# Two streamed matmuls on TensorE ahead of the wait for a normalised input, in a post-norm decoder on one core

## The reference

```
x = _layernorm(x + L0_attn(x))        # 16 heads, Gaussian-splat weights, softmax
x = _layernorm(x + L0_xattn(x, ctx))  # 16 heads of 16, 120 context tokens
x = _layernorm(x + L0_ffn(x))         # 8 experts, the best one per token
x = _layernorm(x + L1_attn(x))        # causal, 16 heads of 16
x = _layernorm(x + L1_xattn(x, ctx))  # two attentions of 16 heads of 32, each with
                                      # its own norms, gains and a GELU layer 256-1024-256
x = _layernorm(x + L1_ffn(x))         # 16 small experts, the best four per token
```

## Time and profile before

| | |
|---|---|
| time, median of 3 runs | 3850.71 us (3845.12 to 3853.26) |
| profiled execution: its time | 3838.08 us |
| profiled execution: span from first to last instruction | 3836.4 us |
| mean granted TensorE clock | 0.916 of full |
| TensorE matmuls busy / weight loads busy | 86% / 61% of the span |
| VectorE, ScalarE, GpSimd busy | 72%, 55%, 25% |

### The profile page before, as it was taken

One profiled execution on the slowest core, in us unless ns is written; L12 is line 12 of the kernel. 1 busy time (PEld: TensorE's weight loads), 2 busy tenths in 40 slices (PEclk: granted clock), 3 DMA queues, 4 the chain that ended last, 5 costly groups with the idle time before them and its releaser, 6 DMA issues. The chain is left out here.

```text
span 3836.4 us, 94561 instructions
## 1 busy us (share of the span) xinstructions
PE 3284.4 (86%) x38960; PEld 2338.5 (61%) x38960; DVE 2751.5 (72%) x6299; ACT 2092.8 (55%) x4222; POOL 972.9 (25%) x1792
## 2 busy tenths in 40 slices
PE   1989888889888888988988888899988898988886
PEld 1666565666666656656656666566655665766654
DVE  5777776777776767777767667677776677777754
ACT  4745665455456564564465555645555556466552
POOL 0312341122223321131133122212342113124310
PEclk9999998999989999989989898898988999998987
DMA  5000000000000000000000000000000000000000
GB/s 168 3 3 2 2 3 5 10 8 3 2 2 4 5 3 7 7 3 2 7 2 2 5 4 8 6 4 2 2 2 3 10 7 6 2 2 2 2 4 6
DMA packets 30365, 31.49 MB, mean 8 GB/s; under 512 B 8673, under 2 KB 26482, under 8 KB 29938
## 3 DMA queue, kind: packets, MB, share of 16 engines
q1 hardware_dynamic: 29938, 25.44, 2.1%
HBM read 21.24 MB, written 4.19 MB: 7 GB/s over the span
## 5 line engine op out<-in xcount | busy, mean ns | idle before, releaser
L1116 ACT ACTIVATE p<-bank,p_log 128x512 f32<-128x512 f32 (+2 forms) x1280 | 746.8, 583 | 1225.3 <-PE bank L808 1174.7
L1690 POOL TENSOR_TENSOR prob<-p,prob 120x256 f16<-120x256 f32 (+2 forms) x512 | 452.6, 884 | 1727.6 <-ACT prob L1117 1726.5
L1117 ACT ACTIVATE prob<-bank,p_log 128x512 f16<-128x512 f32 (+2 forms) x1280 | 747.5, 584 | 0.0
L1392 DVE TENSOR_REDUCE negm<-bank 128x2 f16<-128x512 f32 (+1 forms) x1280 | 675.5, 569 | 24.8 <-PE bank L763 13.5
L1310 DVE TENSOR_TENSOR prob<-p,prob 128x512 f16<-128x512 f32 (+2 forms) x768 | 467.2, 616 | 169.6 <-ACT prob L1117 165.6
L785 PE MATMUL bank<-q,k 32*128 32x256 f16 (+2 forms) x6144 | 486.9, 284 | 69.6 <-ACT prob L1117 26.6
L675 PE MATMUL bank<-w_exp,ident_h 128*128 128x512 f16 x1280 | 418.7, 411 | 16.3 <-DVE xa L1304 11.9
L1699 POOL TENSOR_SCALAR_AFFINE_SELECT probm<-prob 128x128 f16<-128x128 f16 x1024 | 326.3, 357 | 316.4 <-DVE prob L1310 316.4
L785 PEld LDWEIGHTS bank<-q,k 32*128 32x128 f16 (+1 forms) x6144 | 303.5, 108 | 147.1 <-issue 41.4
L808 PE MATMUL bank<-ident_h,negm 128*128 128x256 f16 (+2 forms) x2560 | 376.8, 268 | 0.0
L1682 POOL TENSOR_TENSOR rstd<-veps,minus_half 128x2 f32<-128x2 f32 (+2 forms) x192 | 146.0, 760 | 813.5 <-DVE veps L1278 812.9
(11 more groups left out here) (302 smaller groups left out, 6211.6 us busy)
## 6 DMA issues: line engine op xcount, KB each, us to landing
x<-in_x SPq DMA_DIRECT2D x16, 256.0 KB, 2.7
out<-z SPq DMA_DIRECT2D x16, 256.0 KB, 2.1
xa<-in_li SPq DMA_DIRECT2D x9, 256.0 KB, 4.4
x<-in_li SPq DMA_DIRECT2D x7, 256.0 KB, 4.4
z<-in_wq SPq DMA_DIRECT2D x4, 256.0 KB, 4.1
z<-in_li SPq DMA_DIRECT2D x4, 256.0 KB, 4.6
cx<-in_ctx_t SPq DMA_DIRECT2D x16, 60.0 KB, 1.9
cx<-in_ctx SPq DMA_DIRECT2D x16, 60.0 KB, 1.8
```

The costliest lines, as they stand in the source:

```text
L1116: act(p32[0:n, g % PBUF32, 0:cols], ps[0:n, 0:cols], ACT.Exp, bias=p_log[0:n, :], scale=a.scale)
L1117: act(prob[0:n, 0, g % PBUF, 0:cols], ps[0:n, 0:cols], ACT.Exp, bias=p_log[0:n, :], scale=a.scale).then_inc(a_done, one(a_done))
L1392: v.tensor_reduce(negm[:, h * NT:(h + 1) * NT], ring_v[bank_of(e, v_full)][:, :].rearrange("p (t n) -> p t n", t=NT)[:, :, 0:ATTNS[k].keys ...
L1690: g.tensor_tensor(prob[0:n, 1, m % PBUF, 0:cols], p32[0:n, m % PBUF32, 0:cols], prob[0:n, 0, m % PBUF, 0:cols], ALU.subtract).then_inc(pp_ ...
```

## The change

`STREAM_NORM` goes from 0 to 2, and `transposes` uses it: when the source is a normalised activation, TensorE issues two streamed matmuls into the bank it has just taken, and only then waits for the first token tile. The four transposes overwrite the bank. The wait for the bank, in `slot`, still comes before the streamed matmuls.

```diff
-STREAM_NORM, STREAM_GATES, STREAM_HEADS, STREAM_ROWS = 0, 0, 0, 2
+STREAM_NORM, STREAM_GATES, STREAM_HEADS, STREAM_ROWS = 2, 0, 0, 2
...
                     if after is not None:
                         stream(ps, meanwhile)
                         e.wait_ge(*after)
+                    if normed is not None:
+                        stream(ps, STREAM_NORM)
                     for t in range(NT):
                         if normed is not None:
                             e.wait_ge(normed, upcoming(e, normed))
```

## The result

The kernel after the change takes 3865.56 us (median of 14 runs, 3854.29 to 3875.17), the one before 3850.52 us (14 runs). The ratio is 1.0032, 95% interval 1.0024 to 1.0040: slower by 0.32%, some 12 us, and clear of the 0.2% (the two medians are 15.0 us apart). Forecast were 3856 us, with "slower" as the likeliest of the three signs (0.39); the time lies inside the range, and in the upper half of the range given for the likeliest case. The rise was forecast at 5 us and is 12 to 15.

The account below looks back on a forecast made before the run. TensorE was taken as first suspect for the bound, but not alone. 25 us of exposed cost less 17 us of clock gain, less 2 us, gave +6 us; forecast 3856 us (+0.1%), range 3824 to 3888 us.

Parts of the forecast that it names:

- "slower": Whole kernel: the sign for a time above 3858 us, beyond 0.2% of 3851; chance 0.39.
- the likeliest case: Whole kernel: cost and clock gain nearly cancel, 3856 us, own range 3840 to 3874; chance 0.40.
- the sum: Whole kernel: 25 us cost less 17 us clock gain, less 2 us, giving +6 us.
- (a): Rival, calls without a norm wait: the cost is nearly all on the path, +33 us, 3884 us; chance 0.23.
- (b): Rival, behind the long waits: the clock decides, half the long falls go, -26 us, 3825 us; chance 0.21.
- (c): Rival, whole kernel: TensorE isn't the bound and the cost vanishes, -9 us, 3842 us; chance 0.16.
- The cost term: TensorE in calls without cover: 42.5 us of added work, of which 25 us reach the end.
- 70 calls without a norm wait: Calls whose transposes don't wait for the norm: 0.55 us a streamed pair, 38.5 us of TensorE.
- 0.6: Share of a microsecond added to TensorE that moves the end, where TensorE doesn't wait; read from the chain that ended last.
- the long waits: 30 waits of 1.6 to 4.0 us in "xT" of k = 4 and the tail: pair fits, direct cost 0.
- The clock term: TensorE behind norm waits: fewer falls to 1.2 GHz, 13 us (long waits) plus 4 us (short), 17 us gained.
- the short waits: At most 28 norm waits, 2 us or less: 4 us of pairs uncovered; 4 us clock gain from 15 of them.

Follow-up runs that it names:

- e10: The changed kernel, unedited, run again against the kernel before; ratio 1.0037 (1.0023 to 1.0051).
- e2: Changed kernel with two streamed matmuls only in the 96 calls other than "xT" of k = 4 and the tail, against the kernel before; 0.9998.
- e11: Changed kernel with two streamed matmuls only in the 64 calls of k = 1 to 3, against the kernel before; ratio 1.0021.
- e1: Changed kernel with two streamed matmuls only in the 32 "xT" calls of k = 4 and the tail, against the kernel before; ratio 1.0003.
- e3: Changed kernel with eight streamed matmuls only in the 32 "xT" calls of k = 4 and the tail, against the kernel before; ratio 0.9994.
- e9: The kernel before, unedited, as a kernel of its own against the runs of before; ratio 1.0010 (0.9994 to 1.0025).
- e8: Changed kernel with four streamed matmuls only in the 64 calls of k = 1 to 3, against the kernel before; ratio 1.0047.
- e5: Changed kernel with eight streamed matmuls only in the 16 "xT" calls of k = 4, against the kernel before; ratio 0.9999.
- e6: e3 with eight more streamed matmuls in the tail ahead of the wait for the gates, against the kernel before; ratio 0.9974.
- e12: e6 with four streamed matmuls in the 32 "xoT" calls as well, against the kernel before; ratio 1.0017.
- e4: Changed kernel with four streamed matmuls in all 128 calls, against the kernel before; ratio 1.0077.

## Why the prediction came out as it did

*The places of cost and gain.* Right in kind. The change costs TensorE time where no wait hides it and lifts the clock a little; both are in the profile after, and cost outweighs gain, as the sum said. No rival took over. (a) wanted +33 us, against 12 to 15 in the medians and 18.4 in the profile; (b) wanted the mean clock at 0.93, and it is 0.921; (c) wanted waits for other things to shrink, and they didn't.

*The cost term.* 25 us were taken. Once the clock is out, 25 are in the executions of e10, and 29 to 31 in the two profiles after. The total was right, its distribution wasn't, so that there is luck in it. I charged 70 calls without a norm wait alike, at 0.6, and the long waits nothing. By the table, two matmuls in the 64 early calls cost 15 us; their price is 64 x 0.55 = 35 us, less the 9.9 us that left the waits for `x` 25, so that 0.6 came out there. In the 32 "xoT" calls, 17.6 us at that price, they cost about 1 (e2 less e11). And pairs in the long waits, booked at a direct cost of 0, have 9 us in the table (e1), as a cost or as a clock that was worth less than its price. The 0.6 itself was read from a chain that covers a tenth of the span.

*The clock term.* This is the step that was mis-sized: 17 us were booked, 11 to 12 came. The number of falls avoided agrees, 5 of 30 against 0.14 x 30, though some went without a pair in their call (e2: 3 of 30). It was also read from a miscount: of the 15 stretches of the earlier trace rows six are at 1.00 and seven at 0.57 to 0.79 (0.79 five times, 0.68, 0.57), not five and eight; with seven the sum would have been 2 us larger. Their worth was wrong. I set the whole difference of clock against TensorE's busy time, 3.0 us a fall; the executions of the kernel before give 0.30 us for each microsecond at the lower level, and a stretch of 8 us at 0.56 holds 7 us of that, 2.1 us. Worse, 16 of the 30 are in the tail, where e3's profile gave back behind the tail what it gained in it. TensorE's busy share behind the wait (6.90 of 8 us in the earlier trace rows) looked like a bound; VectorE's 6.16 of 8 in the same row was the warning. In all, the clock gave back 11 us in the profile and 12 in e10's executions. Its places were off too: pairs in the long waits gave 7 us where 13 were booked (e1), pairs in the early calls, which hold the short waits, 8 where 4 were (e11).

*The sum.* 25 - 12 = 13 us over e10's executions, where 25 - 17 - 2 = 6 were forecast: 5 us are the clock term, 2 the deduction for a 0.6 "likely too high", which no row bore out. The first profiles differ by 18 us, because the one of before had less of the lower clock than its kernel usually has (e9).

*The measure of headroom.* The Trainium skill (Perfetto Trace Analysis, Identifying the Most-Contended Engine) would judge TensorE's headroom by the busy share of its weight loads (61%) and by the share of its peak arithmetic that the kernel reaches, and not by the 86%. Read as the prediction read it, that the added work would stay hidden, it didn't come true for the whole kernel: e11 and e8 are 8 and 18 us slower although the clock gave something back. In the "xoT" calls most of the added time was hidden.

*Still open:* by what the time of the "xoT" calls is made good before the long wait, why the halves of the change raise the clock by more than the whole does, what the 9 us of e1 are, and what became of the 12 us that e5's profile gained behind k = 4's waits.

## What to carry to other kernels

Ask of each place, not of the kernel, whether the engine is the bound there: the same two matmuls cost next to nothing in an "xoT" call and 15 us in 64 early ones. Before a wait is filled, look for the next wait behind it, for a faster engine arrives there earlier and may idle, and lose its clock, at a worse place (e3 against e6). And before differences of some 20 us are read out of one profile of each kernel, set span against granted clock over all executions of the unchanged one: here that line explained why one half of a change seemed to cost nothing (e2).

## What the runs showed of the hardware

Two executions of one program differed by 26.4 us in 3850, and the granted clock of TensorE goes with it: 29 of 256 stretches differ in their time at the lower level and hold 24.8 us, the other 227 are alike within 1.6 us in sum. Over 88 executions of this kernel on three chips a microsecond at the 1.2 GHz level cost 0.30 us, and with that taken out the chips agree within 3 us. A higher mean clock is no measure of a faster kernel: 0.937 went with 1.0017 (e12), 0.931 with 1.0077 (e4) and with 0.9994 (e3), 0.935 with 0.9974 (e6).
